# VectorE gates each expert tile when it is ready, with expert numbers made from counts alone, register loads placed early, and transposes one tile ahead

## The reference

```python
logits = x @ Wg + bg
probs = jax.nn.softmax(logits, axis=-1)
top_v, top_i = jax.lax.top_k(probs, TOP_K)
top_v = top_v / (top_v.sum(axis=-1, keepdims=True) + 1e-06)
...
for e in range(NUM_EXPERTS):
    h = jax.nn.silu(x @ W1[e] + b1[e]) * (x @ W3[e] + b3[e])
    out = out + combine[..., e:e + 1] * (h @ W2[e] + b2[e])
x = x + out
```

## Time and profile before

| what | value |
|---|---|
| median of 3 runs | 162.56 us (162.53 to 163.21) |
| the profiled execution, its own time | 163.61 us |
| its span, first to last instruction | 161.9 us |
| granted TensorE clock, share of full speed | 0.999 |
| TensorE busy (matmul) | 146.7 us, 91% of the span |
| TensorE busy (weight load) | 137.4 us, 85% |
| VectorE busy | 103.0 us, 64% |
| ScalarE busy | 76.9 us, 47% |
| GpSimd busy | 85.6 us, 53% |

### The profile page before, as it was taken

One profiled execution on the slowest core, in us unless ns is written; L12 is line 12 of the kernel. 1 busy time (PEld: TensorE's weight loads), 2 busy tenths in 40 slices (PEclk: granted clock), 3 DMA queues, 4 the chain that ended last, 5 costly groups with the idle time before them and its releaser, 6 DMA issues.

```text
span 161.9 us, 4080 instructions
## 1 busy us (share of the span) xinstructions
PE 146.7 (91%) x1217; PEld 137.4 (85%) x1217; DVE 103.0 (64%) x318; ACT 76.9 (47%) x214; POOL 85.6 (53%) x106
## 2 busy tenths in 40 slices
PE   6988896999999999897899898999997999999980
PEld 6977785779998999886778798999997999999970
DVE  0536699989899967987769764364633635665030
ACT  3078356857464694730633336335343445352031
POOL 3640002948553685304810897777777777987000
PEclk9999999999999999999999999999999999999999
DMA  4999895030000004038770298767337998401364
GB/s 145 315 311 290 218 163 92 6 107 26 2 2 4 0 0 130 18 108 265 238 216 12 65 313 300 249 186 256 117 115 231 344 324 278 133 20 49 116 159 130
DMA packets 23821, 24.50 MB, mean 151 GB/s; under 512 B 2525, under 2 KB 16713, under 8 KB 23801
## 3 DMA queue, kind: packets, MB, share of 16 engines
q1 hardware_dynamic: 20608, 20.57, 43.0%
q0 software_dynamic: 1440, 2.82, 5.9%
q10 hardware_dynamic: 1753, 0.87, 2.0%
HBM read 19.91 MB, written 4.33 MB: 150 GB/s over the span
## 4 chain that ended last, share of the span: by engine, by line
PE 54%; POOL 13%; DVE 10%; ACT 9%; issue 8%; DMA 3%; ACTq 1%; POOLq 0%; DVEq 0%
PE psum L1375 15%; PE psum L1436 8%; PE psum L1388 7%; POOL y_scratch L581 6%; PE psum L1418 5%; PE psum L1185 4%; POOL early L604 3%; DMA y_back<-y_scratch 3%; POOL g_room L572 2%; PE psum L1151 2%; PE psum L1153 2%; PE psum L1152 2%; DVE prob L848 2%; DVE negmax L843 2%; ACT g_room L650 2%
## 5 line engine op out<-in xcount | busy, mean ns | idle before, releaser
L1375 PE MATMUL psum<-probT,w 128*128 128x128 f32 x368 | 45.6, 277 | 2.8 <-issue 1.4
L1375 PEld LDWEIGHTS psum<-probT,w 128*128 128x128 f32 x368 | 43.0, 192 | 4.0 <-issue 2.1
L750 ACT ACTIVATE prob<-psum,bias_col 128x128 f32<-128x128 f32 x92 | 26.3, 368 | 37.8 <-PE psum L1375 37.8
L1095 DVE SCALAR_TENSOR_TENSOR probT<-psum,bias_col,prob 128x128 f32<-128x128 f32 x92 | 26.0, 344 | 28.1 <-ACT prob L750 27.4
L572 POOL DMA_INDIRECT g_room<-xf_scratch,idx x22 | 22.2, 1010 | 19.2 <-DVE idx L1029 7.6
L529 POOL TENSOR_TENSOR prob<-prob,rowsum 128x1232 f32<-128x1232 f32 x8 | 18.0, 2252 | 23.6 <-DVE rowsum L839 23.6
L1388 PE MATMUL psum<-w,probT 128*128 x184 | 25.1, 279 | 0.2
L1388 PEld LDWEIGHTS psum<-w,probT 128*128 128x128 f32 x184 | 22.6, 191 | 0.8 <-issue 0.6
L1436 PE MATMUL psum<-vo,probT 128*128 128x128 f32 (+1 forms) x160 | 19.3, 276 | 0.0
L1436 PEld LDWEIGHTS psum<-vo,probT 128*128 128x128 f32 (+1 forms) x160 | 18.5, 192 | 0.0
L581 POOL DMA_INDIRECT y_scratch<-xnT,out_row x16 | 15.8, 986 | 4.7 <-issue 4.1
(11 more groups left out here) (185 smaller groups left out, 209.8 us busy)
## 6 DMA issues: line engine op xcount, KB each, us to landing
w<-in_L_ffn_W_dram SPq DMA_DIRECT2D x54, 256.0 KB, 4.6
early<-in_L_xattn_W_kv_dram SPq DMA_DIRECT2D x2, 512.0 KB, 6.1
y_scratch<-zero_rows SPq DMA_DIRECT2D x2, 512.0 KB, 8.2
x_sb<-in_x_dram SPq DMA_DIRECT2D x2, 256.0 KB, 4.8
early<-in_L_xattn_W_q_dram SPq DMA_DIRECT2D x1, 512.0 KB, 5.9
early<-in_L_xattn_W_out_dram SPq DMA_DIRECT2D x1, 512.0 KB, 8.5
early<-in_L_ffn_b_dram SPq DMA_DIRECT2D x1, 512.0 KB, 5.1
xf_scratch<-xf SPq DMA_DIRECT2D x2, 256.0 KB, 2.6
```

What stands on the lines that cost most here:

```text
L750: act.activation(silu[:, j % 2, c, :], psum[:, 2 * (j % 2), c * P:(c + 1) * P], ACT.Silu, bias=bias_col[:, 0, bass.ds(expert, 1), c]).then ...
L1095: dve.scalar_tensor_tensor(out=hT[:, j % 2, c, :], in0=psum[:, 2 * (j % 2) + 1, c * P:(c + 1) * P], scalar=bias_col[:, 1, bass.ds(expert[j ...
L1375: ins = pe.matmul(psum[:, 2 * (j % 2) + a, c * P:(c + 1) * P], w13[:, j % WR, a, c * P:(c + 1) * P], xt[:, j % XR, :], start=True, stop=True)
```

## The change

- VectorE: gated(0) comes before the ranks of group 2. The bases of the experts are split off other_tiles (other_bases) and come with the expert numbers right behind gated(0). Then gated(1), bias_down(0), ranks, blocks, other_tiles, one-hots, gated(2), and only then other_rows, of which the scatter rows are split off (other_out_rows, behind gated(3)). The wait for the b2 rows moves to bias_down(0). Register loads for tiles 0 and 1 stand before the index read of the first tiles, that for tile 2 behind the expert numbers.
- TensorE: the register loads come out of up; tiles 0 and 1 behind slot_rows of the first tiles (with six warm-up transposes in place of eight), each later one behind the up before it. slot_rows of the other tiles comes behind up(3) in place of expert_xT(4). From tile 5 on the transpose is one tile ahead in place of two.
- ScalarE copies the transposes in the new order.

GpSimd's and SyncE's lists are unchanged.

```diff
@@ scalar
             for j in range(2, NT):
-                if j + 1 < NT and j == 2:
+                if j == 2:
+                    expert_xT(3)
+                gate_silu(j)
+                if j == 2:
+                    expert_xT(4)
+                elif 4 <= j < NT - 1:
                     expert_xT(j + 1)
-                gate_silu(j)
-                if j + 2 < NT:
-                    expert_xT(j + 2)
@@ vector
-            def other_tiles():
-
-                link(dve.tensor_copy(floor_2[:, PAIRS_1:T * K], floors[:, PAIRS_1:T * K]))
+            def other_bases():
+
+                dve.wait_ge(rk_mm, G)
                 link(dve.scalar_tensor_tensor(out=padded[:, :], in0=TOTALS[1], scalar=ROUND_128, in1=taken_r[:, :],
                                               op0=ALU.add, op1=ALU.subtract))
                 link(dve.tensor_tensor(low_pad[:, :, 0:E], lower[:, :, :], over_pairs(padded[:, :], E), ALU.mult))
                 link(dve.tensor_reduce(base[:, :], low_pad[:, :, :], AX.X, ALU.add))
+
+            def other_tiles():
+
+                link(dve.tensor_copy(floor_2[:, PAIRS_1:T * K], floors[:, PAIRS_1:T * K]))
...
                 dve.tensor_scalar(idx[:, FULL:NT], OTHER_AT, row_base[:, 0:1], None, ALU.add).then_inc(idx_ok, 1)
+
+            def other_out_rows():
+
...
+            expert = {}
+
+            def load_expert(j):
+
+                dve.wait_ge(*((eid_1_ok, 1) if j < FULL else (eid_ok, 1)))
+                expert[j] = dve.value_load(eid[0:1, j:j + 1], min_val=0, max_val=E - 1)
...
             first_tiles()
+            load_expert(0)
+            load_expert(1)
             dve.wait_ge(idx_1_mm, 1)
...
             top_two(2)
-            ranks(2)
-            blocks_of(2)
-
-            dve.wait_ge(eid_1_ok, 1)
-            dve.wait_ge(ld["bias"], 16)
-            expert = {}
 
             def gated(j):
 
-                if j == FULL:
-                    dve.wait_ge(eid_ok, 1)
-                expert[j] = dve.value_load(eid[0:1, j:j + 1], min_val=0, max_val=E - 1)
+                if j not in expert:
+                    load_expert(j)
...
             gated(0)
+            other_bases()
+            other_experts()
+            load_expert(2)
+            gated(1)
+            dve.wait_ge(ld["bias"], 16)
+            bias_down(0)
+            ranks(2)
+            blocks_of(2)
             other_tiles()
             one_hots(2)
-            gated(1)
+            gated(2)
             other_rows()
-            other_experts()
-            bias_down(0)
-            for j in range(2, NT + 1):
+            bias_down(1)
+            gated(3)
+            other_out_rows()
+            bias_down(2)
+            for j in range(4, NT + 1):
                 if j < NT:
                     gated(j)
                 bias_down(j - 1)
-                if j == 3:
+                if j == 4:
                     direct_tokens()
@@ tensor
+            def load_expert(j):
+
+                pe.wait_ge(*((eid_1_ok, 1) if j < FULL else (eid_ok, 1)))
+                expert[j] = pe.value_load(eid[0:1, j:j + 1], min_val=0, max_val=E - 1)
+
             def up(j, between=None):
 
-                if j == FULL:
-                    pe.wait_ge(eid_ok, 1)
-                expert[j] = pe.value_load(eid[0:1, j:j + 1], min_val=0, max_val=E - 1)
                 pe.wait_ge(xt_ok, j + 1)
...
             slot_rows(FIRST * K, hit_1, FIRST_AT, hit_1_ok, idx_1_mm)
-            warm_up(8, WARM)
+            load_expert(0)
+            load_expert(1)
+            warm_up(6, WARM)
             direct_xT()
             tokens_x2T(2)
             pe.wait_ge(ld["experts"], 16 * E)
-            pe.wait_ge(eid_1_ok, 1)
             up(0, lambda: logits(2))
             warm_up(4, WARM)
             expert_xT(1)
             count_ranks(2)
             up(1)
+            load_expert(2)
             expert_xT(2)
             down(0)
             expert_xT(3)
             up(2)
+            load_expert(3)
             expert_xT(4)
+            down(1)
+            up(3)
+            load_expert(4)
             slot_rows(T * K, tile_hit, OTHER_AT, hit_ok, idx_mm)
-            down(1)
-            for j in range(3, NT + 1):
+            down(2)
+            for j in range(4, NT + 1):
                 if j < NT:
                     up(j)
-                if j + 2 < NT:
-                    expert_xT(j + 2)
+                if j + 1 < NT:
+                    load_expert(j + 1)
+                    expert_xT(j + 1)
                 down(j - 1)
```

## The result

Four executions of the changed kernel took 167.10 to 167.95 us, median 167.36; beside them the kernel before took 162.55. The ratio is 1.0286 (95% interval 1.0256 to 1.0317): slower by 4.8 us, twice the forecast loss and above the upper end of the range. In ratios here, executions more than 1.5% above the fastest of their kernel are left out (one each of the runs with diagonals last before and rows first, three of the one with the hole alone).

The account below looks back on a forecast made before the run. GpSimd's unbroken 60.7 us from gather 5, which waits for VectorE's index read, was taken to bound the kernel. That read coming 2.4 us later, with stretch and tail unchanged, made 162.56 + 2.4 = 165.0 us, range 163.4 to 166.2.

Parts of the forecast that it names:

- What bounds the kernel: From gather 5 to the last scatter GpSimd runs 60.7 us without a hole, after VectorE's index read; then a fixed tail.
- VectorE's two loads ahead of the first index read: VectorE behind key_in: the pair of register loads takes 1.5 us and delays the read by 1.05 us (0.4 to 1.3).
- TensorE's two early loads: TensorE ahead of direct_xT: the loads lie beside its wait for VectorE's one-hots and cost nothing while VectorE is later.
- Two warm-up transposes less: TensorE's warm-up ahead of direct_xT: six transposes in place of eight change nothing, since TensorE waits there.
- From the logits to the index read: VectorE's reordered steps from top_two(2) at 79.65 us to L1029, the read for the gathers, at 90.9 in place of 88.47.
- The sum: Gather 5 moves from 88.96 to 91.4 us, GpSimd's stretch and tail unchanged: +2.4 on the median 162.56, giving 165.0.
- Gain of TensorE: TensorE's up(4) could start about 91.3 us in place of 93.08, 1.7 us won but lost to later gathers.
- TensorE sets the end: Rival, faster: with GpSimd's chain squeezed by 4 us, TensorE's 1 to 1.7 us would show, about 161.3; chance 0.06.
- The loads are free: Rival: the early loads run beside the steps ahead of them and pass nothing on, +1.4, 163.95 us; chance 0.15.
- More than the index read is late: Rival: VectorE's wait for the gate gather and late gathers for TensorE push the end to 166.3 us; chance 0.12.

Follow-up runs that it names:

- diagonals last before: Kernel before the change, with GpSimd's eight gate diagonals moved behind the last scatter: 161.39 us, ratio 0.9872.
- rows first: Changed kernel with other_rows, the index read that gather 5 waits for, put ahead of gated(2) in place of behind it: 165.40 us, ratio 1.0118.
- the hole alone: Kernel before, with only TensorE's register loads of tiles 0 and 1 put ahead of six warm-up transposes in place of eight: median 164.49 us, ratio 1.0061.
- Diagonals last: Changed kernel with GpSimd's eight gate diagonals moved from behind scatter 15 to behind the last scatter: 161.28 us, ratio 0.9876.
- Filling the hole: Changed kernel with 20 warm-up transposes ahead of TensorE's two early register loads in place of 6 behind them: 165.82 us, ratio 1.0177.
- with the loads covered: Changed kernel, TensorE's early loads behind ten warm-ups, VectorE's loads singly behind first_one_hots, gated(0) and gated(1): 164.81 us, ratio 1.0113.

## Why the prediction was right in its direction and wrong in its size

- *What bounds the kernel*: right. Gather 5's start, 60.7 us of GpSimd without a hole and a tail; measured 61.0 and a tail from the end of the last scatter of 12.5 (before 12.3). Diagonals last shows it from the other side: 5.1 us out of the stretch, 6.1 us less time.
- *VectorE's two loads ahead of the first index read*, +1.05: measured +1.05, and 1.10 at gather 5 when they are covered.
- *TensorE's two early loads*: this is the step that failed. It said "TensorE's two early loads lie beside this wait: free, as long as VectorE is the later one". VectorE was the later one, and direct_xT started when forecast (2.90 behind key_in; with the clock held, rows first shows TensorE waiting 0.31 us for it). What the step left out is what an idle TensorE is granted next: behind the 1.12 us the clock was halved and direct_xT took 2.83 us in place of 1.60. The step beside it, "Two warm-up transposes less: nothing, TensorE waits there", put them at nothing without asking what busy work in that place does for the clock; their number alone was not tested. Of the six profiles with the hole five show the fall, of the eight without it none. Filling the hole takes 1.22 us off gather 5; in time it took 167.36 to 165.82, 1.54, which is back inside the stated range.
- *From the logits to the index read*: right, part by part: forecast 90.9 - 79.65 = 11.25 us, measured 18.77 - 7.65 = 11.12, and no part is off by more than 0.25. Against before, with the loads covered, the order costs 1.15 at gather 5, of which up to 0.52 are what is left of the loads.
- *The sum*: +2.4 forecast, +3.47 at gather 5: 1.1 for VectorE's loads, 1.22 for the clock, 1.15 for the order. GpSimd's stretch (0.34) and the tail (0.26) make 4.07. That leaves 0.7 to the measured 4.8. The profiled execution of before was 1.06 above its median and that of after 0.2 below, and I had put the difference of one profile on the median; the start stage, up to key_in, moves by this much between executions (72.0 to 73.2 us among the profiles shown here), so the 0.7 is within what a single profile leaves open. The clock's 1.22 alone would have made the forecast 166.2, the upper end of the range; the stretch and the tail, which it put at unchanged, and the open 0.7 make the other half of the miss of 2.4.
- *Gain of TensorE*, up(4) from 93.08 to 91.3, "not kept": up(4) came at 91.71, 19.32 behind key_in where before it was 19.92, so only 0.6 of the 1.8; the late logits took the rest. Then TensorE waits 0.74 us for gather 5, as forecast.
- *The rivals*: "TensorE sets the end" was priced at 161.3 if GpSimd's chain were squeezed by 4 us; squeezed by 5.1 it gives 161.28. That the figures meet is luck: the price was a gain of 1 to 1.7 us that the change gives TensorE, and the kernel before, squeezed the same way, comes out level with the changed one. "The loads are free" is refuted for both engines. "More than the index read is late" named later waits; one showed, VectorE's for the gate gather (1.1 us, none before), but it held nothing up: GpSimd has no wait beyond its 0.30 us.

The Trainium skill (TensorE: Matmul & The Clock Gate, Part 1: The HAM clock gate) says that the engine's recent activity sets its clock and that the monitor's time doesn't start with the kernel, so that one kernel differs between runs. The runs agree: one kernel, the changed one with the diagonals last, has executions at a mean clock of 0.989 and of 1.000, and after the same hole of 1.11 to 1.12 us direct_xT took 2.83 us in the changed kernel, 2.57 in the kernel with the hole alone and 1.60 in the run with rows first. Nothing here tells in advance in which execution it falls; the changed kernel's four executions, at a mean clock of 0.963 to 0.965, are alike.

## What to carry to other kernels

A register load that looks free because its engine has to wait anyway was not free on TensorE: it turned busy waiting into idle waiting, and the work behind it ran at half the clock in five of six profiles. Keep the warm-up matmuls ahead of the load (direct_xT took 1.57 to 1.61 us in all six profiles that had ten or twenty there) and check the granted clock of that stretch in a window view. A load moves its hold to where it is put: the pair held VectorE for 1.59 us at either place. Behind an instruction of about 1 us it left 0 to 0.37 us of a hole, so put it there. And where one list runs without a hole to the end, try first to take something out of that list: eight diagonals moved behind it brought 6.1 us in the changed kernel and 1.3% in the kernel before, while the reordering of three other engines cost 4.8 us by itself and seems to pay only behind that and with its loads covered.

## What the runs showed of the hardware that was not expected

- An idle stretch of 1.11 to 1.15 us on TensorE (in the changed kernel behind 1.4 us in which it was busy for 0.77) was followed by some 3 us at 1.2 GHz, in five of the six profiles with that hole; direct_xT took 2.32 to 2.93 us there, and 1.60 in the sixth, the run with rows first.
- With the clock low, the twelve matmuls took 2.83 us in place of 1.60, 1.77 times, not 2; in the window of their last part the granted clock was 0.58, so some of it was at the full clock again.
- Two register loads in a row on VectorE held their follower for 1.59 us, on TensorE for 1.11 to 1.15.
